# The second product of a feed-forward layer: its inputs in pieces of 128, 128 and 96 rows in place of 4 times 88, the attention's tile in the same PSUM bank

## What is computed

```python
def fp4_linear(x, w):
    xq = fp4_quant_dequant(x)          # blocks of 16 along the last dim
    wq = fp4_quant_dequant(w)
    return jnp.einsum('bsk,nk->bsn', xq, wq)
gate = fp4_linear(x, w_gate)           # w_gate, w_up: (352, 128)
y = fp4_linear(x, w_up)
h = jax.nn.silu(gate) * y              # 352 values a token
return fp4_linear(h, w_down)           # w_down: (128, 352)
...
x = x + _L0_attn_ref(xn, ...) + _L0_ffn_ref(xn, ...)
```

## Time and profile before

| | |
|---|---|
| median of 3 runs | 856.14 us (852.33 to 856.45) |
| the profiled execution's own time | 856.67 us |
| its span | 854.9 us |
| PE busy | 799.1 us (93%), 4516 matmul instructions |
| DVE busy | 703.4 us (82%) |
| ACT busy | 694.6 us (81%) |
| POOL busy | 53.8 us (6%) |
| DMA | 99.90 MB, nearly all of it in the experts' loop |

### The profile page before, as it was taken

The page is one execution under the profiler, slowest core; times in us unless marked ns, Lnnn a source line. Parts: engine busy times, 40 slices in busy tenths (PEclk is TensorE's granted clock), DMA queues, the critical chain, the costliest instruction groups (busy, mean ns, idle before and its releaser), DMA issues.

```text
span 854.9 us, 15979 instructions
## 1 busy us (share of the span) xinstructions
PE 799.1 (93%) x4516; PEld 516.5 (60%) x4516; DVE 703.4 (82%) x1523; ACT 694.6 (81%) x1165; POOL 53.8 (6%) x71
## 2 busy tenths in 40 slices
PE   3858899999989889999999999999999999999997
PEld 2521222322222269767888888888888888888885
DVE  5788844356687858749999999999999999999997
ACT  2869999999998955748888888888888888888885
POOL 1620000000000000000000000000000000000000
PEclk9969999999999999999999999999999999999999
DMA  4000000000000000049788888887888888778883
GB/s 125 1 1 0 2 1 1 2 1 1 1 1 1 2 2 13 1 137 216 199 209 203 198 212 201 202 209 200 203 207 202 202 203 208 202 198 213 200 205 91
DMA packets 66778, 99.90 MB, mean 117 GB/s; under 512 B 29270, under 2 KB 45942, under 8 KB 66742
## 3 DMA queue, kind: packets, MB, share of 16 engines
q1 hardware_dynamic: 66742, 99.44, 47.1%
HBM read 97.04 MB, written 2.36 MB: 116 GB/s over the span
## 4 chain that ended last, share of the span: by engine, by line
PE 70%; DVE 16%; ACT 7%; issue 4%; DVEq 2%; DMA 1%; SPq 0%; ACTq 0%
PE PS L1488 9%; PE PS L1490 9%; PE PS L1481 9%; PE PS L1482 9%; PE PS L1483 9%; PE PS L1489 9%; PE PS L1175 5%; ACT E L454 5%; PE PS L1161 2%; PE PS L1224 2%; PE PS L1460 1%; PE PS L1463 1%; PE PS L1297 1%; DVE qy L689 1%; DVE qy L691 1%
## 5 line engine op out<-in xcount | busy, mean ns | idle before, releaser
L589 ACT ACTIVATE SI<-PS 128x512 f32<-128x512 f32 x320 | 191.7, 599 | 79.2 <-PE PS L1483 78.8
L454 ACT ACTIVATE E<-PS 128x1536 f32<-128x1536 f32 x171 | 233.9, 1494 | 11.9 <-PE PS L1161 11.7
L1064 DVE TENSOR_TENSOR HM<-SI,CWB 128x512 f32<-128x512 f32 x320 | 221.3, 691 | 16.7 <-ACT SI L589 0.7
L1069 DVE TENSOR_TENSOR HLo<-HM,HH 128x512 fp32r<-128x512 f32 x320 | 223.0, 697 | 0.1
L395 ACT ACTIVATE HH<-HM 128x512 fp32r<-128x512 f32 x320 | 199.4, 623 | 0.3 <-DVE HM L1064 0.2
L1175 PE MATMUL PS<-E,VS 128*32 128x512 f32 x1024 | 138.6, 622 | 4.0 <-DVE OS L769 3.0
L1481 PE MATMUL PS<-XH,wgH 128*128 128x512 f32 x320 | 133.1, 416 | 0.0
L1488 PE MATMUL PS<-HH,wdH 128*128 128x512 f32 x320 | 128.1, 400 | 0.9 <-DVE HLo L1069 0.9
L1490 PE MATMUL PS<-HH,wdL 128*128 128x512 f32 x320 | 126.4, 395 | 0.0
L1483 PE MATMUL PS<-XH,wgL 128*128 128x512 f32 x320 | 126.3, 395 | 0.0
L1482 PE MATMUL PS<-XL,wgH 128*128 128x512 f32 x320 | 126.2, 394 | 0.0
(11 more groups left out here) (221 smaller groups left out, 870.6 us busy)
## 6 DMA issues: line engine op xcount, KB each, us to landing
CWB<-combine_weights SPq DMA_DIRECT2D x320, 256.0 KB, 4.0
wg_raw<-in_L_ffn_w_gate_dram SPq DMA_DIRECT2D x80, 64.0 KB, 3.8
wd_raw<-in_L_ffn_w_down_dram SPq DMA_DIRECT2D x80, 64.0 KB, 3.6
X<-in_L_attn_x_dram SPq DMA_DIRECT2D x4, 256.0 KB, 3.7
combine_weights<-CWT SPq DMA_DIRECT2D x2, 512.0 KB, 2.9
out_dram<-X SPq DMA_DIRECT2D x4, 256.0 KB, 2.9
combine_weights<-CWT SPq DMA_DIRECT2D x2, 128.0 KB, 3.7
qkvw_raw<-in_L_attn_qkv_w_dram SPq DMA_DIRECT2D x1, 192.0 KB, 3.9
```

What stands on the lines that cost most here:

```text
L454: nc.scalar.activation(E[:, g % RING, 0:w, :], PS[:, 3 * (g % 2):3 * (g % 2) + w, :], ACT.Exp, scale=SCALE0).then_inc(S["exp_act"], 1)
L589: nc.scalar.activation(SI[:, slot % 2, :], bank(4 + slot % 2), ACT.Silu).then_inc(S["s_act"], 1)
L1064: TT(HM[:, slot % 4, :], SI[:, slot % 2, :], CWB[:, q, half, CH * c:CH * c + CH], ALU.mult)\
L1069: TT(HLo[:, slot % 4, :], HM[:, slot % 4, :], HH[:, slot % 4, :].bitcast(F32), ALU.subtract)\
```

## The change

The 352 hidden values of a token are cut into 128, 128 and 96 (`DA = 2` whole pieces and a rest `DR = 96`). A tile's transposes are then three, and the attention's becomes the fourth, in the same bank between the whole pieces and the rest. ACT copies the three column blocks of 128 rows in one instruction and the block of 96 rows in a second, both to `hT`; `aoT` goes. The product takes two pieces with `dnT`, then `outT`, then the rest. `down_T` has three transposes and `down_weights` two copies.

```diff
--- before.py
+++ after.py
@@ -38,6 +38,7 @@
 
     I0 = w_gate.shape[0]
     FP, FA = 88, I0 // 88
+    DA, DR = I0 // P, I0 % P
     BLK = 16
     GRID_MAX = 6.0
     MAGIC = 1.5 * 2.0 ** 22
@@ -133,15 +134,14 @@
 
         outT = sb("outT", [P, D], F32, ph0)
         AO = sb("AO", [P, B, NB, NHG, HG * HD0], F32, ph0)
-        dnT = sb("dnT", [FP, FA, P], F32, ph0)
+        dnT = sb("dnT", [P, DA + 1, P], F32, ph0)
         pre = ExitStack()
         QK1 = sb("QK1", [P, 2, GT * 32, HD0], F32, pre)
         HL = sb("HL", [P, 2, GT, 2, H0, 2, HD0], F16, pre)
         Q4 = sb("Q4", [P, 2, GT, H0, 4, HD0], F16, pre)
         pre.close()
         HF = sb("HF", [P, NT, I0], F32, ph0)
-        hT = sb("hT", [FP, 2, FA, P], F32, ph0)
-        aoT = sb("aoT", [P, 2, P], F32, ph0)
+        hT = sb("hT", [P, 2, DA + 2, P], F32, ph0)
         ph0.close()
         QK = [QK0[:, 0], QK0[:, 1], QK1[:, 0], QK1[:, 1]]
         XQ, XQT = Hn, HT
@@ -502,8 +502,9 @@
                 act.wait_ge(S["ffT_pe"], t + 1)
                 if t >= 2:
                     act.wait_ge(S["ff_pe"], t - 1)
-                copy(hT[:, t % 2, :, :], bank(4 + t % 2)[0:FP, :].rearrange("p (a n) -> p a n", a=FA))
-                copy(aoT[:, t % 2, :], bank(6 + t % 2)[:, 0:P]).then_inc(S["ffT_act"], 1)
+                src = bank(4 + t % 2).rearrange("p (a n) -> p a n", a=DA + 2)
+                copy(hT[:, t % 2, 0:DA + 1, :], src[:, 0:DA + 1, :])
+                copy(hT[0:DR, t % 2, DA + 1, :], src[0:DR, DA + 1, :]).then_inc(S["ffT_act"], 1)
                 if t % GT == 1 and t > GT:
                     roots(B + t // GT, range(t // GT * GT - GT, t // GT * GT))
                 if t % GT == 0 and t >= 2 * GT:
@@ -778,8 +779,9 @@
                 nc.vector.tensor_copy(guT[:, w, :], filled("w", w)[:, 0:I0]).then_inc(S["shade_dve"], 1)
 
             def down_weights():
-                src = filled("w", 2)[0:FP, :].rearrange("p (a n) -> p a n", a=FA)
-                nc.vector.tensor_copy(dnT[:, :, :], src).then_inc(S["shade_dve"], 1)
+                src = filled("w", 2)[:, 0:(DA + 1) * P].rearrange("p (a n) -> p a n", a=DA + 1)
+                nc.vector.tensor_copy(dnT[:, 0:DA, :], src[:, 0:DA, :])
+                nc.vector.tensor_copy(dnT[0:DR, DA, :], src[0:DR, DA, :]).then_inc(S["shade_dve"], 1)
 
             def inputs_T(g):
                 nc.vector.tensor_copy(XQT[:, CH * g:CH * g + CH], filled("x", g)).then_inc(S["shade_dve"], 1)
@@ -1209,8 +1211,9 @@
             def down_T():
                 o = bank_free("w", 2)
                 pe.wait_ge(S["fw_dve"], 1)
-                for a in range(FA):
-                    last = TR(o[0:FP, P * a:P * a + P], dn_raw[:, FP * a:FP * a + FP], ident[:, :])
+                for a in range(DA):
+                    TR(o[:, P * a:P * a + P], dn_raw[:, P * a:P * a + P], ident[:, :])
+                last = TR(o[0:DR, P * DA:P * DA + P], dn_raw[:, P * DA:I0], ident[:, :])
                 last.then_inc(S["shade_pe"], 1)
 
             def inputs_T(g):
@@ -1283,20 +1286,22 @@
             def ff_T(t):
                 if t >= 2:
                     pe.wait_ge(S["ffT_act"], t - 1)
-                for a in range(FA):
-                    TR(bank(4 + t % 2)[0:FP, P * a:P * a + P], HF[:, t, FP * a:FP * a + FP], ident[:, :])
+                o = bank(4 + t % 2)
+                for a in range(DA):
+                    TR(o[:, P * a:P * a + P], HF[:, t, P * a:P * a + P], ident[:, :])
                 b, k = t // NB, t % NB
-                TR(bank(6 + t % 2)[:, 0:P], AO[:, b, k, :, :].rearrange("p n w -> p (n w)"), ident[:, :])\
-                    .then_inc(S["ffT_pe"], 1)
+                TR(o[:, P * DA:P * DA + P], AO[:, b, k, :, :].rearrange("p n w -> p (n w)"), ident[:, :])
+                TR(o[0:DR, P * (DA + 1):P * (DA + 2)], HF[:, t, P * DA:I0], ident[:, :]).then_inc(S["ffT_pe"], 1)
 
             def ff_mm(t):
                 pe.wait_ge(S["ffT_act"], t + 1)
                 if t >= 2:
                     pe.wait_ge(S["x1_dve"], t - 1)
-                for a in range(FA):
-                    MM(bank(t % 2)[:, 0:D], hT[:, t % 2, a, :], dnT[:, a, :], start=(a == 0), stop=False)
-                MM(bank(t % 2)[:, 0:D], aoT[:, t % 2, :], outT[:, :], start=False, stop=True)\
-                    .then_inc(S["ff_pe"], 1)
+                o = bank(t % 2)[:, 0:D]
+                for a in range(DA):
+                    MM(o, hT[:, t % 2, a, :], dnT[:, a, :], start=(a == 0), stop=False)
+                MM(o, hT[:, t % 2, DA, :], outT[:, :], start=False, stop=False)
+                MM(o, hT[0:DR, t % 2, DA + 1, :], dnT[0:DR, DA, :], start=False, stop=True).then_inc(S["ff_pe"], 1)
 
             def x_T(g):
```

## The result

| | before | changed |
|---|---|---|
| median (lowest to highest), 20 runs each | 853.99 us (851.80 to 856.60) | 851.88 us (849.91 to 853.82) |
| ratio | | 0.9977, 95% interval 0.9966 to 0.9987 |
| the profiled execution's own time, its span | 856.67, 854.9 us | 853.13, 851.4 us |
| first transpose of the stage to x_T(2) | 29.74 us | 27.29 us |
| in front of the stage | 308.26 us | 307.00 us |

The change gains 0.23%, 2.1 us, where 0.27% and 2.3 us were forecast; that is under 0.5%, the case held likeliest. The interval of the ratio allows a gain of 1.1 to 2.9 us, so the whole time says that there is a gain and roughly how much, no more. (Over 20 runs the kernel before is 2.15 us faster than the median of the three that the forecast started from.

The account below looks back on a forecast made before the run. PE looked like the bound of the feed-forward's second product, with DVE already setting the stage's end. Cumulative shifts of -0.44, -1.44, -1.66, -1.99 and -2.32 us gave -2.3 us from 856.14: 853.8 us, range 850.5 to 856.4.

Parts of the forecast that it names:

- A tile's price: Feed-forward's second product: 12 PE instructions a tile instead of 15, saving 0.33 us at PE's pace.
- ACT's copies: Each tile's two copies take 384 and 128 columns instead of 512 and 128, 0.11 us less.
- The square root sets group 0: In the stage's first four tiles, ACT's first square root, later than DVE's work, decides: -1.66 us.
- DVE paces groups 1 and 2: Later tiles follow DVE's list; only instructions saved in front of tiles 8 and 12 count: -1.99, then -2.32 us.
- The three waits of PE: PE waits about 1.0, 0.9 and 1.4 us for DVE's norms before transposing each of the three groups.
- The weight in the attention: One transpose less and two dnT copies on DVE instead of one: taken as 0, ends -0.15 and +0.60 us.
- Behind x_T(2): Everything after the last group's normed transposes, routing and then experts, moves as a block.
- The time: Whole kernel: 2.3 us off the 856.14 us median of three runs, giving 853.8 us, 0.27%.
- Rival 1: Stage's transposes are paced by columns, not count: 0.22 us a tile, 1.5 us in all, 854.6 us; chance 0.12.
- rival 2: PE's whole relief reaches the stage's end: 5.4 us, 850.7 us; chance 0.08.
- Rival 3: PE's new waits before the normed transposes make the clock fall: +7.4 us, 863.5 us; chance 0.05.
- rival 4: No visible change, from drift in the attention or costlier dnT copies: 855 to 857 us; chance 0.13.

Follow-up runs that it names:

- the late relief: Changed kernel without the rest piece (one transpose, one product) in tiles 9 to 11 and 13 to 15; stage 27.24 us against 27.29.
- the norm on ACT: Changed kernel with the second norm, Hn, of groups 0 to 2 moved from DVE to ACT; stage 24.62 us, time 850.73 us, ratio to before 0.9968.
- the five transposes: Changed kernel with one redundant transpose of 32 hidden values more in each tile; stage 28.05 us against 27.29.
- the best version: Changed kernel with Hn of groups 0 to 2 on ACT and one 512-column copy a tile; 850.04 us, ratio to before 0.9946.

## Why the prediction was right

The steps that carry the 2.3 us are there, in their order and nearly in their size. The agreement of the whole time, 2.1 us against 2.3, is better than 20 runs can show, and so in part luck. Step by step, times from the stage's first transpose:

| step | before | changed | moved | forecast |
|---|---|---|---|---|
| x1(0) | 3.04 | 2.62 | -0.42 | -0.44 |
| x1(3) | 8.03 | 6.62 | -1.41 | -1.44 |
| after the first root | 10.88 | 9.26 | -1.62 | -1.66 |
| x_T(0) | 14.73 | 13.10 | -1.63 | -1.66 |
| x1(8) | 17.52 | 15.56 | -1.96 | -1.99 |
| x_T(1) | 22.30 | 20.20 | -2.10 | -1.99 |
| x1(12) | 25.04 | 22.65 | -2.39 | -2.32 |
| x_T(2) | 29.74 | 27.29 | -2.45 | -2.32 |

- *A tile's price.* 0.33 us, right: spacing 1.33.
- *ACT's copies.* The pair takes 0.65 us as forecast; x1(0) came 0.02 less early than summed.
- *The square root sets group 0.* Right, with 0.43 us of wait left on DVE and PE's wait for tile 6's copy as forecast (0.4 us; recorded 0.39 in front of its weight load).
- *DVE paces groups 1 and 2.* Right in kind, and shown by the late relief and by the norm on ACT. The sum is 0.13 us short. Before and, last line, after:

```profile
330.08 0.34 DVE L665 TENSOR_SCALAR Hn<-X,mv,ir 128x128 f32<-128x128 f32 x1
330.56 0.60 PE L1309 MATMUL PS<-ident,XN 128*128 128x128 f32 x4
...
336.31 0.34 DVE L665 TENSOR_SCALAR Hn<-X,mv,ir 128x128 f32<-128x128 f32 x1
336.63 0.29 DVE L959 TENSOR_TENSOR X<-X,PS 128x128 f32<-128x128 f32 x1
```

```profile
326.81 0.34 DVE L666 TENSOR_SCALAR Hn<-X,mv,ir 128x128 f32<-128x128 f32 x1
```

The last norm of group 1 moved from 21.82 to 19.81, by 2.01 us and so as forecast. But before, x_T(1) had not waited for it: PE came to it 0.14 us after that norm's end, now it starts 0.05 after it, so x_T(1) moved by 2.10. Of that 0.04 was lost up to x1(12). And DVE's last list, taken as free of waits, held 0.06: 0.32 us from 336.31 to 336.63, where it is 0.26 now. That is 0.11 - 0.04 + 0.06. DVE's own need from x1(8) to x1(11) was put too high as well, 4.6 us where 4.50 were measured, since a recorded idle of 0.35 starts at the end of the record in front and the next instruction usually starts before that end; no x_T waited for x1(11), so the stage doesn't show it.
- *The three waits of PE.* There, 1.0, 0.9 and 1.4 us by the start of instructions forecast; measured 320.10 - 319.03 = 1.07, 327.20 - 326.24 = 0.96 and 334.29 - 333.01 = 1.28 from the last product's second instruction to x_T. That PE stays over 90% busy was right for the first part (14.71 of 16 us) and not for the second (9.62 of 11.3, 85%); the clock stayed at 1.00.
- *The weight in the attention.* Costed at nothing. The two copies take this, which answers to the earlier trace rows:

```profile
86.60 0.42 DVE L783 COPY dnT<-PS 128x256 f32<-128x256 f32 x1
86.94 0.28 DVE L784 COPY dnT<-PS 96x128 f32<-96x128 f32 x1
87.14 0.68 DVE L770 COPY OS<-PS 128x512 f32<-128x512 f32 x1
```

From 86.60 to 87.14 are 0.54 us where one copy had 0.60, so it gained 0.06 if anything; too little to be found in the time.

- *Behind x_T(2).* The rest moved as a block, within 0.2 us in the changed kernel's trace (516.9 and 517.1), though that part itself scatters by more, as its repetition shows (517.6). The experts' loop took 460.7 us in both.
- *The time.* The start was the weak point: the median of three runs stood 2.15 us above that of twenty. The range had to cover that and did.

Rival 1 fell with the five transposes, rival 2 with the late relief. Rival 3 did not occur: with waits of about 1 us in front of the x_T the clock stayed at 1.00 in every trace that has them. The one fall seen in the stage, in another kernel, lay at its start and cost 1.63 us, not the 9.7 that rival 3 would have cost before the gain is taken off (the clock stayed low for 3.4 us and not to the end of the stage). Of rival 4 the scatter is real, 4 us between runs, and over 20 runs the gain stands clear of it.

## What to carry to other kernels

Before removing work from the busiest engine of a stage, follow the list of the second one through it in order: here 5.3 us came off TensorE and 2.45 us arrived at the end of the stage, because from the first square root on VectorE had its own list to do and waited for TensorE only 0.82, 0.35 and 0.52 us. Price fp32 transposes and products that move 128 columns by their number and not by width or depth, as these runs show for transposes of 32 to 128 values and sums over 88 to 128; then cutting a length into the fewest pieces is the gain. And once one engine has been relieved, an edit on the other that was worth 0.76 us may be worth 2.67.

## What the runs showed of the hardware

- The clock fell to 1.2 GHz for 3.4 us at the start of the stage in one of two executions of one kernel, after stretches in which PE did the same in both (busy 0.63 us of the 2 in front of the stage, then 0.99 of 1.46). Such falls in the last 60 us of the attention go with the start of the stage, over the twelve traces with the new pieces: 303.38 and 304.35 us with none, 304.60 to 305.95 with one, 306.82 and 307.00 with two.
- The experts' loop, in which PE is recorded 100% busy, was not of one length: from the first to the last start of its first gate product 460.7 us before and in the changed kernel, 461.3 in the same kernel again, and 463.1 in the best version, with the granted clock at 1.00 in every window from 500 to 800 us that I read of them. It doesn't scatter freely: in the eleven traces with Hn on DVE it is 460.7 to 461.3 us, and in the three with Hn on ACT 461.3, 462.1 (on the kernel before) and 463.1. In these three the starts fall behind the changed kernel's from the first expert to the last, a little in each: 0.5, 1.4 and 2.4 us in all, 1.0 of the last at the beginning. So the move of the norm seems to cost something in a loop that it doesn't touch. I found no cause, and this stays open. It is the size of the gain in question, and it is why the best version's profile ends later (849.0 us) than its stage would have it.
